# One token-block kernel on one core: a product turned round, factors and a rotation moved by transfers, inverse roots by a power, new instruction orders

## The reference, cut to what matters

```
a: y = mamba_block(x)                      # in_proj, conv, scan in 2 chunks, gate, rms norm,
                                           # out_proj, + x, layer norm, then one more norm -> x1
b: q, k = x1 @ w_q, x1 @ w_k               # 8 heads of 64, causal attention
   g = softmax(x1 @ w_gate) over 8 experts # per head: the largest wins (top 1), weight g
   v = sum over the chosen expert of (x1 @ value_experts[e, h]) * g
   o = softmax(q k^T) v                    # per head
   out = sum_h,e (chosen e) g * o_h @ output_experts[e, h]   # + x1, norm -> x2
c: linear attention with rotary embedding on x2, + x2, two norms -> x3
d: x3 through 64 experts of 32 slots each with soft dispatch and combine (all tokens)
```

## Time and profile before

| what | value |
|---|---|
| median of 3 runs | 1497.77 us (1497.28 to 1497.99) |
| the profiled execution, its own time | 1495.65 us |
| its span | 1493.8 us |
| PE busy | 1434.7 us, 96% |
| DVE busy | 1205.2 us, 81% |
| ACT busy | 820.6 us, 55% |
| POOL busy | 748.6 us, 50% |
| mean granted TensorE clock | 0.98 |

### The profile page before, as it was taken

The page is one execution under the profiler, slowest core; times in us unless marked ns, Lnnn a source line. Parts: engine busy times, 40 slices in busy tenths (PEclk is TensorE's granted clock), DMA queues, the critical chain, the costliest instruction groups (busy, mean ns, idle before and its releaser), DMA issues. The chain is left out here.

```text
span 1493.8 us, 32591 instructions
## 1 busy us (share of the span) xinstructions
PE 1434.7 (96%) x10940; PEld 1267.7 (85%) x10940; DVE 1205.2 (81%) x2359; ACT 820.6 (55%) x1850; POOL 748.6 (50%) x1833
## 2 busy tenths in 40 slices
PE   8789999999999999999999999988999999898998
PEld 6658888888888888888888887867999999898998
DVE  6778889889888898898898887768888888757664
ACT  4354555454555464455555544306776777667775
POOL 1433346346355354454453451226777777467772
PEclk8889999999999999999999999998999999999999
DMA  5100000000000000000000004007777777887872
GB/s 194 61 8 8 1 15 2 14 16 1 15 15 2 16 5 12 15 5 12 16 1 15 8 1 128 2 3 174 196 193 193 191 192 195 264 315 297 312 304 75
DMA packets 135426, 130.43 MB, mean 87 GB/s; under 512 B 7232, under 2 KB 125248, under 8 KB 128768
## 3 DMA queue, kind: packets, MB, share of 16 engines
q1 hardware_dynamic: 135296, 128.79, 27.9%
HBM read 72.93 MB, written 55.84 MB: 86 GB/s over the span
## 5 line engine op out<-in xcount | busy, mean ns | idle before, releaser
L737 PE MATMUL ps_l<-ve_f,oe 128*128 128x128 f32 x2048 | 275.7, 279 | 0.8 <-DVE ve_f L1740 0.8
L737 PEld LDWEIGHTS ps_l<-ve_f,oe 128*128 128x128 f32 x2048 | 248.8, 192 | 23.1 <-issue 20.4
L1740 DVE SCALAR_TENSOR_TENSOR ve_f<-ps_s,oT 128x512 f32<-128x512 f32 x248 | 166.7, 681 | 4.1 <-PE ps_l L737 2.3
L2934 POOL TENSOR_TENSOR d_s<-d_ex 128x1024 f32<-128x1024 f32 x31 | 125.2, 4040 | 83.0 <-ACT d_ex L2684 82.8
L1701 DVE COPY_PREDICATED vals<-oh,ps_l 128x1024 f32<-128x1024 int32 x112 | 146.9, 1312 | 19.3 <-PE ps_l L477 17.4
L2559 PE MATMUL ps_s<-d_ex,arena 128*128 128x128 f32 x1024 | 121.1, 277 | 4.6 <-DVE d_ex L2827 4.6
L2559 PEld LDWEIGHTS ps_s<-d_ex,arena 128*128 128x128 f32 x1024 | 118.2, 194 | 5.0 <-DVE d_ex L2827 5.0
L2547 PE MATMUL ps_l<-arena 128*128 (+1 forms) x960 | 114.5, 279 | 3.9 <-ACT d_raw L2679 3.9
L1293 ACT ACTIVATE ve_f<-ps_l,r 128x128 f32<-128x128 f32 x128 | 47.3, 370 | 125.9 <-DVE r L1713 125.6
L2547 PEld LDWEIGHTS ps_l<-arena 128*128 128x128 f32 x960 | 111.9, 195 | 4.1 <-ACT d_raw L2679 4.1
L475 PE MATMUL ps_l<-veH,x1H 128*128 128x512 f32 x256 | 115.2, 450 | 0.1
(11 more groups left out here) (332 smaller groups left out, 3842.7 us busy)
## 6 DMA issues: line engine op xcount, KB each, us to landing
logits<-d_raw SPq DMA_DIRECT2D x128, 256.0 KB, 3.5
e_lt<-logits SPq DMA_DIRECT2D x32, 1024.0 KB, 5.1
y_slots<-d_ys SPq DMA_DIRECT2D x64, 256.0 KB, 4.6
d_ex<-y_slots SPq DMA_DIRECT2D x8, 1024.0 KB, 6.9
e_y<-y_slots SPq DMA_DIRECT2D x6, 1024.0 KB, 7.2
d_w<-W SPq DMA_DIRECT2D x16, 256.0 KB, 3.4
arena<-xT SPq DMA_DIRECT2D x16, 128.0 KB, 2.4
arena<-x SPq DMA_DIRECT2D x16, 128.0 KB, 2.4
```

What stands on the lines that cost most here:

```text
L737: last = pe.matmul(ps_u[:, cols], oe[:, hp, e, :], mo[:, n % MO, hp, :], start=False, stop=(e == NE - 1 and hp == HP - 1), skip_group_chec ...
L1740: V.scalar_tensor_tensor(mo[:, n % MO, :, :].rearrange("p a n -> p (a n)"), chosen_of(b, c), float(NE - e), oT[:, u, c, :, :].rearrange("p ...
L2934: G.tensor_tensor(s8[:], part[:, 0:8, :], part[:, 8:16, :], ALU.add).then_inc(n, 1)
```

## The change

The parts, in the order of the diff:

1. `root` takes the place of `newton` on POOL: two instructions, the second a power with exponent -0.5.
2. `b_rnt` (PE) transposes one 128x32 tile `rn` (factor and expert number of each token and head) into 32 rows, `b_rn` (ACT) copies them out, `spread` (SP) writes them to DRAM (16 KB) and reads them back with two transfers, each of which repeats 8 KB on 64 partitions, into `nb`. `b_rgs`, `b_rgb`, `b_oht`, `b_choice` go. `b_ot` is now an ACT copy of two head pairs at a time, and `b_og` one DVE product of 1024 columns. `b_mo` compares with `nb` in SBUF.
3. `b_out` swaps its operands: the masked outputs are the weights, the experts move. The sum comes out with tokens on the partitions, so `b_oa` and `b_oat` go and `b_res` reads the sum itself. `b_start` becomes four matmuls.
4. `b_vg` goes; `b_pt` scales the turned probabilities by the gate, in two ACT instructions instead of one.
5. For batches below 13 `c_rot` is replaced by `swap`: two transfers within SBUF that exchange even and odd partitions; the sign moved into the sine table.
6. `b_scores` fills both bank pairs, two head pairs at a time. The lists of all engines are reordered.

```diff
+def root(pool, wait_apart, done, k, source, var, eps, half, v, y):
+    wait_apart(pool, source)
+    pool.tensor_scalar(v[:], var, 1.0, eps, ALU.mult, ALU.add).then_inc(done, 1)
+    wait_apart(pool, (done, k + 1))
+    pool.tensor_tensor(y[:], v[:], half[:], ALU.pow).then_inc(done, RSQRT_OPS - 1)
...
+            def spread(b):
+                sp.wait_ge(q["b_rn"], b + 1)
+                wait(sp, q["b_nb"], 32 * (b - 1))
+                sp.dma_start(rn_dram[b % 2].rearrange("a r n -> (a r) n"), rows_s[0:4 * C * HP, :]
+                             ).then_inc(q["b_rn_out"], 16)
+                sp.wait_ge(q["b_rn_out"], 16 * (b + 1))
+                wait(sp, q["b_mo"], OUTS * b)
+                for a in range(2):
+                    sp.dma_start(nb[DH * a:DH * (a + 1), :, :, :, :].rearrange("p q c h n -> p (q c h n)"),
+                                 rn_dram[b % 2, a:a + 1].rearrange("a r n -> a (r n)").to_broadcast([DH, 2 * C * HP * P])
+                                 ).then_inc(q["b_nb"], 16)
+            def swap(b):
+                sp.wait_ge(q["c_q"], b + 1)
+                wait(sp, q["c_qr"], 2 * b)
+                sp.dma_start(t1[0:P:2, :, :], ql[1:P:2, :, :]).then_inc(q["c_swap"], 16)
+                sp.dma_start(t1[1:P:2, :, :], ql[0:P:2, :, :]).then_inc(q["c_swap"], 16)
...
                 for u in range(2):
+                    spread(2 * pair + u - 2)
                     load(2 * pair + u + 1, 1 - u)
+                    swap(2 * pair + u - 3)
                     store(2 * pair + u - 3)
...
+            def b_rnt(b):
+                pe.wait_ge(q["b_rg"], 2 * (b + 1))
+                wait(pe, q["c_x3t"], b - 1)
+                pe.transpose(mixed_home(b)[0:4 * C * HP, 0:P], mixed_of(b), id_f[:]).then_inc(q["b_rn_ps"], 1)
...
-                pe.matmul(ps_u, id_r[:], x1H[:, u, :], start=True, stop=False, skip_group_check=True)
-                pe.matmul(ps_u, id_r[:], x1L[:, u, :], start=False, stop=False,
-                          skip_group_check=True).then_inc(q["b_start"], 1)
+                for c in range(C):
+                    cols = slice(c * P, (c + 1) * P)
+                    pe.matmul(sum_of(b)[:, cols], x1H[:, u, cols], id_r[:], start=(c == 0), stop=False,
+                              skip_group_check=True)
+                    last = pe.matmul(sum_of(b)[:, cols], x1L[:, u, cols], id_r[:], start=False, stop=False,
+                                     skip_group_check=True)
...
-                    last = pe.matmul(ps_u[:, cols], oe[:, hp, e, :], mo[:, n % MO, hp, :], start=False,
+                    last = pe.matmul(sum_of(b)[:, cols], mo[:, n % MO, hp, :], oe[:, hp, e, :], start=False,
...
+            def b_ot(b, u, g):
+                act.wait_ge(q["b_pv"], 2 * b + g + 1)
+                wait(act, q["b_mo"], OUTS * (b - 1))
+                copy(oT[:, u, :, 2 * g:2 * g + 2, :].rearrange("p c h n -> p h c n"),
+                     ps_o.rearrange("p (h c n) -> p h c n", h=2, c=C)).then_inc(q["b_ot"], 1)
...
-                copy(pt[:, s, a, :, :].rearrange("p a b -> p (a b)"), ps_v[0][:, a, 0:3 * P]
-                     ).then_inc(q["b_pt"], 1)
+                act.wait_ge(q["b_gate"], 7 * b + 4)
+                nc.scalar.activation(pt[:, s, a, 0:2, :].rearrange("p a b -> p (a b)"), ps_v[s][:, a, 0:2 * P], ACT.Copy,
+                                     scale=gx[:, 0, h:h + 1])
+                nc.scalar.activation(pt[:, s, a, 2, :], ps_v[s][:, a, 2 * P:3 * P], ACT.Copy, scale=gx[:, 1, h:h + 1]
+                                     ).then_inc(q["b_pt"], 1)
...
+            def b_og(b, u):
+                dve.wait_ge(q["b_nb"], 32 * (b + 1))
+                dve.wait_ge(q["b_ot"], 2 * (b + 1))
+                V.tensor_tensor(oT[:, u, :, :, :], oT[:, u, :, :, :], nb[:, 0, :, :, :], ALU.mult).then_inc(q["b_og"], 1)
...
-                V.scalar_tensor_tensor(mo[:, n % MO, :, :].rearrange("p a n -> p (a n)"), chosen_of(b, c), float(NE - e),
+                V.scalar_tensor_tensor(mo[:, n % MO, :, :].rearrange("p a n -> p (a n)"),
+                                       nb[:, 1, c, :, :].rearrange("p a n -> p (a n)"), float(NE - e),
                                        oT[:, u, c, :, :].rearrange("p a n -> p (a n)"), ALU.is_equal, ALU.mult
                                        ).then_inc(q["b_mo"], 1)
...
             def b_res(b):
-                dve.wait_ge(q["b_oat_ps"], b + 1)
+                dve.wait_ge(q["b_oe"], OUTS * (b + 1))
...
-                dve.wait_ge(q["c_rot_ps"], b + 1)
-                V.tensor_tensor(t1[:], linear_of(b)[:].rearrange("p (a n) -> p a n", a=2),
+                dve.wait_ge(q["c_swap"], 32 * HELD + b - HELD + 1 if b >= HELD else 32 * (b + 1))
```

More of the change, by code:

```diff
@@ L329, in token_blocks @@
             a_op_ps a_r a_xb a_n a_x1t_ps a_x1h a_x1l a_x1
-            b_g_ps b_eg b_gate b_oht_ps b_oht b_qk_ps b_qk b_v_ps b_v0 b_v b_vg b_s_ps b_max b_p b_pt_ps b_pt
-            b_pv b_rg b_rgs b_rgb_ps b_rgb b_ot b_m_ps b_mo b_oe b_oa b_oat_ps b_x2t_ps b_x2t b_start
-            c_qk_ps c_g c_km c_q c_v_ps c_v c_rot_ps c_qr c_t2 c_krt_ps c_kr c_kv_ps c_kv c_out_ps c_z c_res c_n
+            b_g_ps b_eg b_gate b_qk_ps b_qk b_v_ps b_v0 b_v b_s_ps b_max b_p b_pt_ps b_pt
+            b_pv b_rg b_rn_ps b_rn b_rn_out b_nb b_ot b_og b_mo b_oe b_x2t_ps b_x2t b_start
+            c_qk_ps c_g c_km c_q c_v_ps c_v c_swap c_qr c_t2 c_krt_ps c_kr c_kv_ps c_kv c_out_ps c_z c_res c_n
             c_x3t_ps c_x3t c_x3""".split()
@@ L448, in _ @@
             sp.dma_start(oe[:], o_exp).then_inc(experts_in, 16)
-            for b in range(2, 5):
-                load(b, b % 2)
+            load(2, 0)
+            load(3, 1)
+            spread(0)
+            load(4, 0)
+            spread(1)
+            swap(0)
             store(0)
@@ L709, in b_choice @@
-            def b_choice(b, u, c):
-                if c == 0:
-                    pe.wait_ge(q["b_oht"], b + 1)
-                if (b, c) != (Z, 1):
-                    wait(pe, q["b_mo"], OUTS * b + NE * c)
-                else:
-                    wait(pe, q["b_pt"], HB * NB)
-                rows = slice(64 * c, 64 * c + 64)
-                for hp in range(HP):
-                    last = pe.matmul(chosen_of(b, c)[:, hp * P:(hp + 1) * P], pick[rows, hp, :, :].rearrange("p a k -> p (a k)"),
-                                     ohT[rows, u, :], start=True, stop=True, skip_group_check=True)
-                last.then_inc(q["b_m_ps"], 1)
@@ L1068, in _ @@
             b_qk(1, 1, 1)
-            b_pv(0, 3)
-            b_rgb(0, 3)
+            b_pv(0, 1)
             b_qk(1, 1, 2)
             b_qk(1, 1, 3)
+            b_rnt(0)
             b_gates(1, 1)
@@ L2108, in _ @@
             b_v(1, 4)
-            b_mo(0, 0, 0, 1)
+            b_og(0, 0)
+            b_mo(0, 0, 0, 0)
             b_v(1, 5)
@@ L2142, in _ @@
             b_mo(0, 0, 1, 6)
-            b_rg(1, 3)
-            b_ot(1, 1, 2)
             a_ln2(2)
@@ L2157, in _ @@
             slot(NB // 2, 0, False, True, True, True, False)
+            b_res(Y)
+            b_x2(Y, 0)
+            b_og(Z, 1)
             b_mo(Z, 1, 0, 0)
```

811 lines of the change are left out of this document (331 added, 480 removed).

## The result

The changed kernel takes 1437.62 us in the median (1436.34 to 1438.83, 4 runs), the kernel before on the same chip 1497.53 us (1495.52 to 1497.99, 4 runs): ratio 0.9602, 95% interval 0.9586 to 0.9619. That is 60 us less; 31 were forecast, and the range ended 8 us above the measured time. The profiled execution has a span of 1435.2 us, 58.6 less than before. On its page PE is busy 95% of the span, DVE 83%, ACT 57%, POOL 38%.

What follows compares the result with a forecast made beforehand. PE was taken to bound the kernel, DVE a close second. A slot of 57.5 - 2.7 + 0.3 = 55.1 us saves 35 us in all; with the tail's +4, 1464.7 profiled, 1467 us median, range 1446 to 1490.

Steps and rivals of the forecast that it cites:

- PE's parts, -2.7: PE instructions removed and added in one slot sum to -2.7 us, bounds -2.4 and -2.95.
- The sum 57.5 - 2.7 + 0.3: Slot time: old slot, less PE's parts, plus one PE wait, gives 55.1 us, a gain of 2.4 a slot.
- T2: Follow-up theory, not in the prediction: part of the unforecast 2.1 us a slot comes from fewer waits between engines.
- Rival B: New order also closes PE's slow first steps, value products standing together: 1 us a slot more, 1453 down to 1445; 15%.
- PE as the only limit: In the old slot PE is busy 56.96 of 57.20 us and never released late for long; DVE a close second.
- Rival A: DVE and the handoffs are the limit: gain 18 us less the tail's 4, 1484 us, range 1475 to 1493; 20%.
- DVE 48.7: DVE's need in one slot falls from 49.9 to 48.7 us, including 0.2 for `b_mo` with both inputs in SBUF.
- The 0.3 us at the second `b_pv`: PE waits there for the last `b_pt`, some 0.3 us a slot.
- The root, 0.5 to 1 us: The power on POOL takes 0.5 to 1 us in place of about 3.7, with no gain in time.
- The transfers: Factors land in 5.9 us, about 1 us ahead of `b_og`; the swap needs about 2 us; both cost 0.
- Rival C: Slower: 128 copies of one 8 KB row land late at `b_og`, 1 us a slot per us over the slack; 9%.
- The tail, +4: Last batch's factors and products come later, +8.5 us, with 4.5 given back after: net +4 us.

Runs made afterwards that it cites:

- the two runs: Changed kernel with the head pairs of scores and `b_pv` issued apart: ratio 0.9853; changed kernel with four extra half-array visits a slot: ratio 0.9762.
- three edits on PE: Changed kernel with about 0.9 us a slot more PE work at the slot's head, middle (rotation) or end: ratios 0.9689, 0.9661, 0.9701.

## Why the prediction was wrong, point by point

- **PE's parts, -2.7:** right. By starts: rows' transposes -0.98, numbers -0.65, one-hot -0.35, `b_oat` -0.14, rotation -0.86, `b_start` +0.16, `b_rnt` +0.11.
- **The sum 57.5 - 2.7 + 0.3:** the step that failed. It takes every instruction that stays at its old distance to the next. The new order took nine changes of form out of the slot: 1.4 to 1.7 us by the two runs, 1.55 by starts. Beside it by starts: 0.4 on the value products' first steps (not tested by a run), 0.33 of PE's wait for `kr` (all that T2 explains), with some 0.2 given back elsewhere, net. 57.53 - 2.71 - 1.55 - 0.41 - 0.33 + 0.2 = 52.7. In that net stand also the slower steps beside the two visits of the number products, some 0.2 us, which the -0.65 for them doesn't hold. Rival B, at 15% and 1 us a slot, comes nearest, but it named the value products, which are 0.4; the scores and `b_pv`, 1.55, it didn't name. The old rows had both terms: twenty changes could have been counted, and a step of 0.2 to 0.3 ahead of and behind each group read.
- **PE as the only limit:** half right. It is for the new order (three edits on PE cost their full length). In the old one 0.86 us less on PE brought nothing, and 1.2 less on DVE neither. The reading that no row of the stretch has an idle time ended by a releaser was wrong by one row: at 532.82 PE had waited 0.17 us for ScalarE's `kr`. By my own reasoning the rotation alone would have gained 10 us. In the new lists they pay, as the rotation put back there shows (+9 us). Rival A was wrong as well: its idle DVE time shrank from 7.3 to 3.5 us a slot, because `b_res` and `b_x2` stand there now.
- **The Trainium skill's measure** (Perfetto Trace Analysis, Identifying the Most-Contended Engine): the weight loads' share is 88% now and DVE's 93%, so it would still call DVE the limit. The runs say PE; the measurement decides.
- **DVE 48.7:** 49.2 measured. `b_og` took 1.30 to 1.92 (mean 1.8) instead of 1.23 while POOL's `xb` ran beside it (1.72 for 0.73 before), and L1568 takes 1.07 for 0.69. I had this from the Trainium skill's GPSIMD Engine Reference, Key points (contention with VectorE instructions that have two SBUF inputs), as a matter of `b_mo`. The trace agrees, and it matters there who begins first. The `b_mo` at 435.54 begins ahead of POOL's L2134 (435.71) and takes 0.68, L2134 1.67 for 1.27. In the tail the `b_mo` at 901.66 begins behind L2134 (901.50) and takes 1.65, L2134 1.27:

```profile
435.54 0.68 DVE L1672 SCALAR_TENSOR_TENSOR ve_f<-nb,oT 128x512 f32<-128x512 f32 x1
...
901.66 1.65 DVE L1672 SCALAR_TENSOR_TENSOR ve_f<-nb,oT 128x512 f32<-128x512 f32 x1
```

  In the slots no row of PE waits for an instruction that is slowed so.
- **The 0.3 us at the second `b_pv`:** not there; PE has no wait that another engine ended.
- **The root, 0.5 to 1 us:** 0.72, right. "No gain": wrong in kind. It gains nothing as an edit, and the new order loses 8.5 us a slot without it.
- **The transfers:** landing 5.9, right; the swap 2.0, right. The data were to be 1 us ahead of `b_og`; it waits 0.50 for them, in the part of DVE's slot that has slack. Rival C: no.
- **The tail, +4:** mis-sized, +9.2. From the stats of Y, where the slots end now, to those of Z it is 33.1 us; I had 28 from the slot's end. 10.4 of them stand ahead of `b_og` (I had 9.1), and the products took 22.7 for 18.6, of which the clock is 2.1 and the slow `b_mo` at most 1.0. What was given back after it, 4.2 of a forecast 4.5, is right.
- **The range** stopped at 1446, where B took 1 us a slot and little more, although nothing in the profile bounded that term from above: five visits fewer, at some 0.3 to 0.5 us each (an estimate from the old trace's steps around one), are 1.5 to 2.5 us a slot, down to 1432.

## What to carry to other kernels

A list of PE is priced by its instructions and by its changes of form: count the visits to products that use half the rows or columns, read the steps on both sides of one, and put such products together. A part that is taken out of a tuned order can be worth nothing, if what it covered then becomes a wait, as the rotation did; test a part alone in the old order before the gain is booked to it. And a new order can hang on a shorter dependency that gains nothing by itself, as the power did: ask what order it allows.

## What the hardware did that was not expected

- A change of form to or from half-array products costs PE 0.15 to 0.19 us here, and one of the steps it slows is the one between the first two products after the return (0.21 for 0.11). The 128*32 transpose shows no such step.
- The power of 128x2 numbers on GpSimd takes 0.69 to 0.83 us, the root with its first instruction 1.0 to 1.6, where the Newton series took 3.9 to 5.3 us in the trace of before.
- An instruction on DVE with two SBUF inputs can take 1.8 times as long beside an elementwise product on GpSimd (1.21 for 0.69), in one case 2.4 times (1.65 for 0.68), and GpSimd's can be slowed as well (`xb` 1.72 for 0.73). For `b_mo` and L2134 it is the one that begins second.
- 512 KB to 64 partitions, all read from the same 8 KB of DRAM, land in 5.9 us, and half of them in some 2 us less.
